# A two-layer decoder on one core: weight loads in slots, first keys in their own bank, VectorE's normalisation behind both maxima

## The reference

```python
# self-attention, per sequence (128 tokens), 16 heads of width 8
q, k, v = x @ Wq + bq, x @ Wk + bk, x @ Wv + bv
o   = softmax(q k^T / sqrt(8)) v @ Wo + bo
# attention over the past: queries from o, 2 x 256 past states, one softmax for each set
rq, rk, rv = o @ Wrq + brq, past @ Wrk + brk, past @ Wrv + brv
r   = mean over the two sets of softmax(rq rk^T / sqrt(8)) rv
g   = sigmoid([o, r] @ Wg + bg)
y   = layernorm(x + g * r + (1 - g) * o)
# then cross-attention, 16 experts of which the gates choose, gated attention unit,
# one-head attention, 8 experts of which one is chosen, each with a layer norm
```

## Time and profile before

| | us |
|---|---|
| median of 3 runs (875.06 to 891.75) | 875.5 |
| the profiled execution | 875.86 |
| its span | 874.1 |
| PE busy (71%) | 618.0 |
| DVE busy (60%) | 523.5 |
| ACT busy (40%) | 351.3 |
| POOL busy (14%) | 122.5 |

### The profile page before, as it was taken

One profiled execution on the slowest core, in us unless ns is written; L12 is line 12 of the kernel. 1 busy time (PEld: TensorE's weight loads), 2 busy tenths in 40 slices (PEclk: granted clock), 3 DMA queues, 4 the chain that ended last, 5 costly groups with the idle time before them and its releaser, 6 DMA issues.

```text
span 874.1 us, 16404 instructions
## 1 busy us (share of the span) xinstructions
PE 618.0 (71%) x5566; PEld 335.9 (38%) x5566; DVE 523.5 (60%) x1268; ACT 351.3 (40%) x642; POOL 122.5 (14%) x224
## 2 busy tenths in 40 slices
PE   1367887878677776777855777766999677686763
PEld 0144553223222222222322555543444366564552
DVE  2245664666656566565435576556656599667666
ACT  1035553465555465654743454540000223254221
POOL 4011210501010101101122120020000133110000
PEclk9999896699989899898976898956999899798796
DMA  4654220100010000000112222000000000010001
GB/s 128 196 140 106 54 59 1 38 2 1 1 38 2 1 20 18 3 1 1 38 37 67 56 74 76 8 0 1 0 0 0 1 0 1 0 32 12 1 0 48
DMA packets 35404, 27.63 MB, mean 32 GB/s; under 512 B 5894, under 2 KB 34310, under 8 KB 35206
## 3 DMA queue, kind: packets, MB, share of 16 engines
q1 hardware_dynamic: 35340, 26.77, 11.3%
HBM read 8.93 MB, written 1.05 MB: 11 GB/s over the span
## 4 chain that ended last, share of the span: by engine, by line
PE 54%; DVE 16%; issue 13%; ACT 10%; SPq 4%; DMA 1%; DVEq 1%; POOL 0%; ACTq 0%; POOLq 0%
PE banks L1008 8%; PE banks L1492 6%; PE banks L950 5%; PE banks L481 4%; PE banks L990 3%; PE banks L400 3%; ACT probs L617 3%; DVE rec_negmax L1167 3%; SPq L2086 2%; ACT o_T L1102 2%; PE banks L1019 2%; PE banks L1475 2%; PE banks L466 1%; PE banks L1554 1%; DVE o L1184 1%
## 5 line engine op out<-in xcount | busy, mean ns | idle before, releaser
L1167 DVE TENSOR_REDUCE rec_negmax<-banks 128x2 bf16<-128x512 f32 x256 | 167.4, 688 | 106.9 <-PE banks L950 106.4
L1095 ACT ACTIVATE probs<-banks 128x1024 f32<-128x1024 f32 x128 | 131.5, 1027 | 58.7 <-PE banks L990 58.6
L745 DVE TENSOR_REDUCE negmax<-banks 128x8 bf16<-128x1024 f32 x64 | 78.3, 1223 | 85.7 <-PE banks L443 85.5
L1008 PE MATMUL banks<-probs,rV 128*32 128x256 f32 x1024 | 88.7, 420 | 19.8 <-ACT o_T L1102 18.9
L617 ACT ACTIVATE probs<-banks 128x1024 f32<-128x1024 f32 x64 | 65.1, 1017 | 59.8 <-PE banks L466 59.8
L950 PE MATMUL banks<-shared 62*128 62x512 bf16 x256 | 63.5, 422 | 5.3 <-DVE rec_negmax L1167 5.3
L1492 PE MATMUL banks<-shared,w_r 128*128 128x512 f32 x128 | 64.5, 595 | 1.6 <-DVE shared L1525 1.5
L1525 DVE TENSOR_TENSOR shared<-banks,out_T 128x512 f32<-128x512 f32 x64 | 43.6, 690 | 23.4 <-PE banks L1475 23.4
L990 PE MATMUL banks<-shared 64*128 64x256 bf16 x512 | 52.2, 282 | 2.6 <-DMA shared<-rec_neg_T 2.6
L481 PE MATMUL banks<-probs,shared 128*32 128x128 f32 x1024 | 44.6, 296 | 12.0 <-ACT probs L617 11.9
L443 PE MATMUL banks<-shared 62*128 62x128 bf16 x512 | 28.8, 239 | 28.4 <-issue 11.8
(11 more groups left out here) (254 smaller groups left out, 1148.0 us busy)
## 6 DMA issues: line engine op xcount, KB each, us to landing
shared<-qk_parts SPq DMA_DIRECT2D x96, 128.0 KB, 2.4
shared<-rq_parts SPq DMA_DIRECT2D x30, 128.0 KB, 2.5
xk_T<-in_x_T SPq DMA_DIRECT2D x4, 256.0 KB, 3.3
w_r<-in_w_r SPq DMA_DIRECT2D x1, 1024.0 KB, 5.0
shared<-rec_neg_T SPq DMA_DIRECT2D x64, 2.0 KB
xk_T<-in_ctx_T SPq DMA_DIRECT2D x4, 256.0 KB, 3.1
kv_T<-in_ctx_T SPq DMA_DIRECT2D x16, 64.0 KB, 1.8
out<-Y SPq DMA_DIRECT2D x4, 256.0 KB, 2.4
```

Of the source, the lines that this page charges most:

```text
L745: nc.vector.tensor_reduce(c.negmax[:, i % 2, :].rearrange("p (r j) -> p r j", r=2)[:, :, 4 * half:4 * half + 4], c.max_pair.rearrange("p ( ...
L1008: last = self.nc.tensor.matmul(c.ctx_bank[HV * q:HV * (q + 1), past * PAIR:(past + 1) * PAIR], c.rV[:, t, 4 * g + q, :], c.probs[:, i % 4, ...
L1095: nc.scalar.activation(c.probs[:, i % 4, :], c.score_pairs[i % 2], ACT.Exp, scale=HEAD_SCALE)\
L1167: self.nc.vector.tensor_reduce(out, c.max_banks[r].rearrange("p (a t) -> p a t", a=NP_PAST), AX_X, ALU.max, negate=True).then_inc(s["rec_m ...
```

## The change

It does the following.

- **SyncE and ScalarE issue the loads.** load_first keeps two loads (w_qk, b_qk). Four (ident_b, w_v, b_v, ident_f) go to ScalarE's queue as load_turn; TensorE waits for them only ahead of its step loop. The rest is cut in slots of SyncE's step loop, behind rows, queries or keys of a step: load_past (6) in t = 0, load_out (4) in t = 1, three of load_rest's 33 in each of t = 2 to 12 (w_r, 1 MB, in t = 6; gate_rows, 512 KB, in t = 7), and Y (1 MB, still counted in load_rest) in t = 13. rows(0) comes behind load_past.
- **The first group.** The first keys are projected into score_banks[0], without a wait for the queries' bank. ScalarE and VectorE split all of the queries ahead of the keys, and ScalarE issues the six DMAs of the first keys itself. A small Exp on ScalarE and a memset on VectorE stand ahead of them.
- **Slots.** The past keys move from t = 2 to t = 6 (their spread on SyncE from t = 4 to t = 8), the past values from t = 3 to t = 12, the preparation from t = 12 to t = 13; waits are renamed to fit. The two small biases of halves() move to t = 5.
- **VectorE's order.** In the attention steps normalise(t-3) now stands ahead of window(t-1). In the loop over the past both maxima of a step come first, and normalise stands behind them at k = 2, 6, 10, 14 instead of between them at k = 3, 7, 11, 15; add_residual the same at k = 13 instead of 14.

```diff
+def split_bank(c, name, g):
+
+    return c.score_banks[0] if g == 0 and name in ("self_k_", "cross_k_") else c.proj_bank
...
     def project_out(g, *waits):
         pe.wait_ge(*s.after("self_ctx_t", 4 * g + 4))
+        if g == 0:
+            pe.wait_ge(*s.after("load_out", c.n_load_out * 16))
...
     def past_keys():
-        project("past_", 0, c.w_rk[:, :], c.past_T[:, :], ("load_rest", c.n_load_rest * 16), ("self_k_rest", 2))
+        project("past_", 0, c.w_rk[:, :], c.past_T[:, :], ("load_past", c.n_load_past * 16), ("self_k_rest", 3))
 
     def past_values():
-        pe.wait_ge(*s.after("past_rest", 1))
+        pe.wait_ge(*s.after("self_out", 2))
...
-            project_q(t // 4 + 1, *([("past_v", 1)] if t == 4 else [("self_out", t // 4 - 1)] if t > 4 else [("self_k_rest", 1)]))
+            project_q(t // 4 + 1, *([("self_k_rest", 2)] if t == 4 else [("self_out", t // 4 - 1)] if t > 4 else [("self_q_rest", 1)]))
         if t % 4 == 1 and t < 12:
             project_k(t // 4 + 1, ("self_q_rest", t // 4 + 2))
-        if t == 2:
+        if t == 6:
             past_keys()
-        if t == 3:
+        if t == 12:
             past_values()
         if t == 10:
             project_rq(0, ("self_k_rest", 4))
-        if t == 12:
+        if t == 13:
             prepare_pe(c, pe)
         if t == 14:
             project_rq(1, ("prep_d", 1))
         if t in (7, 11):
-            project_out(t // 4 - 1, ("rq_rest", 1) if t == 11 else ("self_k_rest", 3))
+            project_out(t // 4 - 1, ("rq_rest", 1) if t == 11 else ("past_rest", 1))
...
         project_k(0, ("rec_exp", 16 * NPAIR))
-        turn_x(0, ("cross_k_rest", 1))
+        turn_x(0)
         project_q(0)
         turn_x(1, ("cross_q_rest", 1))
     else:
         pe.wait_ge(*s.after("load_first", c.n_load_first * 16))
         project_q(0)
-        project_k(0, ("self_q_rest", 1))
+        project_k(0)
+        pe.wait_ge(*s.after("load_turn", c.n_load_turn * 16))
...
     else:
         act.wait_ge(*s.after("load_first", c.n_load_first * 16))
         high_of("q", 0, 0)
+        middle_act(c, act, "self_q_", 0, c.qk_parts[:, 0], c.left[:, 0, :])
         high_of("k", 1, 0)
-        middle_act(c, act, "self_q_", 0, c.qk_parts[:, 0], c.left[:, 0, :])
         middle_act(c, act, "self_k_", 0, c.qk_parts[:, 1], c.left[:, 1, :])
+        act.wait_ge(*s.after("set_zero", 2))
+        spread_rows(c, act, "self_k_", 0, c.KT[:, 0], c.qk_parts[:, 1], K_ORDER, "self_kt0")
...
+        if t == 5:
             halves()
+        if t == 6:
             rest(c, dve, "past_", 0, c.b_rk[:, 0:1], c.rq_parts[:, 3], c.left[:, 2, :])
-        if t == 3:
+        if t == 12:
             past_v()
-        if t == 12:
+        if t == 13:
             prepare_dve(c, dve)
...
         low_dve(c, dve, "cross_q_", 0, c.qk_parts[:, 0], c.left[:, 0, :])
     else:
         rest_of("q", 0, 0)
+        low_dve(c, dve, "self_q_", 0, c.qk_parts[:, 0], c.left[:, 0, :])
         rest_of("k", 1, 0)
-        low_dve(c, dve, "self_q_", 0, c.qk_parts[:, 0], c.left[:, 0, :])
         low_dve(c, dve, "self_k_", 0, c.qk_parts[:, 1], c.left[:, 1, :])
     for t in range(LAST + 1):
         if t < B:
             maximum(t, 0)
-        if t:
-            window(t - 1)
         if cross and 0 <= t - 4 < B:
             add_out(t - 4)
         if 0 <= t - 3 < B:
             normalise(t - 3)
+        if t:
+            window(t - 1)
         if t < B:
             maximum(t, 1)
             add_v_bias(t)
...
     load(0)
-    if not cross:
-        others(0)
-    load(1)
-    load(2)
     if cross:
+        load(1)
+        load(2)
         keys(0)
         queries(0)
     else:
+        others("first")
+        load(1)
         sp.wait_ge(*s.after("set_zero", 2))
         queries(0)
-        keys(0)
-        others(1)
+        others("rows")
     for t in range(B + 2):
         if 0 <= t - 1 < B:
             rows(t - 1)
@@ -907,11 +918,15 @@
             queries(t // 4 + 1)
         if t % 4 == 3 and t < 12:
             keys(t // 4 + 1)
+        if others:
+            others(t)
+        if t == 0 and not cross:
+            load(2)
         if t == 4:
             load(3)
         if t == 14 and not cross:
             past_queries_sp(c, sp, 0)
-        if not cross and t == 4:
+        if not cross and t == 8:
             spread_rows(c, sp, "past_", 0, c.rKT, c.rq_parts[:, 3], K_ORDER, "past_kt")
...
                 if more:
                     self.maximum(0)
-                if k == 3 and n:
-                    self.normalise(n - 1, 3)
-                if k in (7, 11, 15):
-                    self.normalise(n, k // 4 - 1)
-                if k == 14 and n:
-                    self.add_residual(n - 1)
                 if more:
                     self.maximum(1)
+                if k == 2 and n:
+                    self.normalise(n - 1, 3)
+                if k in (6, 10, 14):
+                    self.normalise(n, k // 4 - 1)
+                if k == 13 and n:
+                    self.add_residual(n - 1)
...
-    pe.wait_ge(*s.after("self_out", 2))
+    pe.wait_ge(*s.after("past_v", 1))
...
+        load_first = [(c.w_qk, "w_qk"), (c.b_qk, "b_qk")]
+        load_turn = [(c.ident_b, "ident_b"), (c.w_v, "w_v"), (c.b_v, "b_v"), (c.ident_f, "ident_f")]
+        load_past = [(c.past_T, "past_T"), (c.w_rk, "w_rk"), (c.b_rk, "b_rk"), (c.w_rv, "w_rv"), (c.b_rv, "b_rv"),
+                     (c.b_g, "b_g")]
+        load_out = [(c.w_o, "w_o"), (c.b_o, "b_o"), (c.w_rq, "w_rq"), (c.b_rq, "b_rq")]
+        load_rest = [(c.ln_w, "ln_w"), (c.w1_raw, "w1_raw"), (c.b1_raw, "b1_raw"), (c.w_g, "w_g"),
...
+                if step == "first":
+                    load_all(sp, load_first, "load_first")
+                elif step == "rows":
+                    sp.wait_ge(*s.after("set_zero_rest", 3))
+                    sp.dma_start(c.KT[63:P:64], a["key_rows"]).then_inc(s["load_rows"], 16)
+                    for past in range(NP_PAST):
+                        sp.dma_start(c.rKT[62 + past:P:64], a["past_rows"][past]).then_inc(s["load_rows"], 16)
+                elif step == 0:
+                    load_all(sp, load_past, "load_past")
+                elif step == 1:
+                    load_all(sp, load_out, "load_out")
+                elif step < 13:
+                    load_all(sp, load_rest[3 * (step - 2):3 * (step - 1)], "load_rest")
+                elif step == 13:
+                    sp.dma_start(c.Y[:, :, :], a["x"].rearrange("b t d -> t b d")).then_inc(s["load_rest"], 16)
...
+            load_all(act, load_turn, "load_turn")
+            act.wait_ge(*s.after("set_warm", 1))
+            nc.scalar.activation(c.warm[:, 1:2], c.warm[:, 0:1], ACT.Exp)
```

More of the change, by code:

```diff
@@ L290, in declare @@
     c.sem = s = Signals(lambda name: ctx.enter_context(nc.semaphore(name)))
-    s.own("load_", "first rest rows")
-    s.own("set_", "memset zero zero_rest bias")
+    s.own("load_", "first turn past out rest rows")
+    s.own("set_", "memset zero zero_rest bias warm")
     s.own("past_", "proj hi rest mid lo kt v_proj v")
@@ L349, in rest @@
         dve.wait_ge(*s.after(name + "lo", g))
[L350 removed]
+    nc.vector.scalar_tensor_tensor(left, split_bank(c, name, g), bias, parts[:, 0, :], ALU.add, ALU.subtract)\
         .then_inc(s[name + "rest"], 1)
@@ L399, in project @@
             pe.wait_ge(*s.after(name_, count))
-        nc.tensor.matmul(c.proj_bank, w, x, start=True, stop=True).then_inc(s[name + "proj"], 1)
+        nc.tensor.matmul(split_bank(c, name, g), w, x, start=True, stop=True).then_inc(s[name + "proj"], 1)
     def project_q(g, *waits):
@@ L727, in halves @@
     def halves():
-        dve.wait_ge(*s.after("load_rest", c.n_load_rest * 16))
+        dve.wait_ge(*s.after("load_past", c.n_load_past * 16))
         nc.vector.tensor_scalar(c.b_rv_half[:, :], c.b_rv[:, :], 0.5, None, ALU.mult).then_inc(s["set_bias"], 1)
@@ L852, in attention_pool @@
             residual(4 * g + 7)
-        if not cross and g == 1:
+        if not cross and g == 2:
             middle_low_pool(c, pool, "past_", 0, c.rq_parts[:, 3], c.left[:, 2, :])
```

32 lines of the change are left out of this document (9 added, 23 removed).

## The result

| | before | after |
|---|---|---|
| median of the runs, us | 875.28 | 808.76 (805.01 to 825.70, 4 runs) |
| ratio of the two, with its 95% interval | | 0.925 [0.917, 0.933] |
| profiled execution, us | 875.86 | 807.19 |
| its span, us | 874.1 | 805.4 |

The account below looks back on a forecast made before the run. No engine was full; TensorE's waits set the time. Savings of 16.3 us in self-attention, 38 of loop idle time, 4 of clock and 1.5 in cross-attention summed to 60, taking 875.86 to 816 us, range 802 to 838.

Parts of the forecast that it names:

- Idle time: Loop over the past: of 45.4 us TensorE idles waiting for normalise and add_residual, 38 go (bounds 19 and 45).
- The clock: Loop over the past: less time at TensorE's low clock, 4 us less (0 to 13).
- the clock recovers: Rival, 13%: all ten low-clock stretches in the loop go, 9 us more, and Y lands in 5.5 us: 805 us.
- First maxima: Start of self-attention: the first maxima come 4.7 us earlier (ends 1.5 and 6), at 17.0 us.
- the contention rival: Rival, 8%: spreads and loads share DMA engines; first keys land 3 us later, step 8's another 2: 821 us.
- The idle 16.92: Self-attention, before the first scores: TensorE's 16.92 us idle, with the first row issued behind loads, goes entirely.
- Past keys out of step 2: Self-attention: the past keys' 1.91 us of matmul leave the path in step 2, 1.2 us less.
- Steps 4 to 8: Self-attention: step 4 0.5 us less, normalise in step 5 0.6 less, the wait for spreads in step 8 2.0 more.
- SyncE's three issues fill its own slack: Self-attention, step 12: three load issues on SyncE use time it has spare, 0.3 us more.
- The wait for Y: Self-attention, step 13: the preparation waits for Y's load, about 4.2 us (3.5 to 5), then one low-clock step, 1.1.
- normalise ahead of rest: Self-attention, steps 5, 9 and 15: TensorE's idle time before the turned product goes, 0.6 us each.
- The slower rival: Rival, 3%: in the loop VectorE stands still in normalise for a late turned context, next maxima queued behind: 916 us.

Follow-up runs that it names:

- Experiment 2: Three variants of the changed kernel's loop: normalise in its old slot ahead of both maxima, 809.78 us; only add_residual moved, 852.41; one normalise of four put back, 828.98.
- experiment 1: Kernel before with only the loop's order changed, 828.34 us; with only attention's normalise moved, 872.25; changed kernel with both orders undone, 869.67.
- Experiment 4: Changed kernel with the first keys' spreads on SyncE's queue, 810.76 us; changed kernel with the past keys' six loads moved to step 1, 813.36.
- the last kernel of experiment 2: Changed kernel with one of four normalise per pair put back between the loop's maxima: 828.98 us in one execution.
- the third kernel of experiment 1: Changed kernel with both VectorE reorderings undone, leaving loads, slots and the first group: 869.67 us, ratio 0.993.
- experiment 3: Changed kernel with Y given its own semaphore, which VectorE waits for at the first add_residual: 808.60 us, ratio 0.922.

## Why the prediction held in sum and missed in its terms

**The loop: 58.7 against 42.** The mechanism was right: normalise and add_residual wait ready-made behind a maximum, and moving them frees the turn. Two terms were too small. *Idle time.* "Of 45.4 us idle in 34 places I leave ... 38 less" failed: 51.0 went. Of the 7 us left for gaps and late maxima only 1.1 is there. And 7.0 more came from a wait that the sum did not hold, the context's product waiting for ScalarE's copy (18.9 to 11.9): 37.9 + 7.5 - 1.1 + 7.0 = 51.3. Experiment 2 ties it to normalise: it stays at 18.9 where only add_residual is moved, is 12.8 with one turn of four late and 11.9 with none. ScalarE's waits before show a way that this can come about (before, then after):

```profile
ACT rec_neg_T L1108 <- PE banks L969: 41.5, 29, 1.5
```

```profile
ACT rec_neg_T L1123 <- PE banks L984: 2.3, 7, 0.4
```

ScalarE stood waiting 41.5 us for the turned maxima, and its exponentials and the copy of the context were queued behind that. That this queue is the way it goes is argued from the rows, not tried. *The clock.* 4 us was taken, with 13 as the end; 7.7 came. The line of the granted clock in 40 slices of the span, before and after, shows it:

```profile
PEclk9999896699989899898976898956999899798796
```

```profile
PEclk9988878599999999999569989569999999697896
```

The loop lies in slices 9 to 20 before, and four of these have an 8. After, slices 9 to 19 are nines throughout. The objection in the rival "the clock recovers", that the low stretches follow the gate product and not a wait, fell: in experiment 1 the low stretches inside the loop went with the waits alone, and in experiment 2 the busy time went up by 3.75 us with eight waits put back.

**Self-attention: 8.9 against 16.3**, by the steps of the prediction:

- *First maxima*, 4.7 less: 2.6 (21.70 to 19.13). ScalarE's queue was priced by its issues, 0.63 each, and these took 0.67. The first maxima were taken as 3.2 us behind the start of the last issue (2.6, and 0.6 for SyncE's loads), and it was 5.1 (14.03 to 19.13). The start at 19.13 is 2.1 later than the 17.0 forecast, where the contention rival had 3. Experiment 4 gives 1.5 for the order with everything on SyncE's queue; what part of it is the second queue is open.
- *The idle 16.92* went entirely, as forecast: 27.2 became 10.2 between first maxima and first scores.
- *Past keys out of step 2*, 1.2 less: by step 4 the gain was 62.96 - 43.07 = 19.9, which leaves 0.3 for it in this pair of profiles (2.0 with the last kernel of experiment 2, whose step 4 is at 41.40). TensorE comes earlier to step 4 and waits there, 4.18 us for 1.12. The prediction named this end for past values in step 3 and should have applied it to step 2 as well.
- *Steps 4 to 8*: 3.0 given back, where 0.9 was forecast (-0.5 - 0.6 + 2.0). TensorE waited 1.76 us at 65.63 for a row, which it did not before, and 4.01 for the spreads in step 8 against 3.36. The waits of 4 us are followed by a step at the low clock (eight products in 0.61 us, not 0.40), here in step 4 too, where the kernel before had 0.40.
- *Steps 8 to 12*: 1.0 given back against a gain of 0.3. The load of cos held SyncE for 2.23 us at 86.56, and the wait at step 12 is 4.19 us for 1.05. "SyncE's three issues fill its own slack" failed there. A load in that place took 1.4 to 1.9 us in the three kernels of experiment 2 too, with waits of 4.1 to 4.2 behind it; in the third kernel of experiment 1 none did, and the wait is 2.17.
- *Step 12 to the loop*: 6.9 given back against 5.9 (1.2 + 5.3 - 0.6).
- *The wait for Y*, 4.2 and 1.1 for the cold step (0.7 + 6.3 - 2.65 is 4.35, so the sum had slipped by 0.15): 5.09, and by experiment 3 it is worth 4.8 with all that follows. Y landed 6.6 us after its issue (6.3 taken).
- *normalise ahead of rest*, 1.8 less: 4 to 6 by itself. The prediction read one wait of 0.65 us and counted three steps; the row over all of self-attention has 6.4 us in 10 places, and 0.7 in one is left. With the loads moved the same waits go (6.0 in 10 places without the order, 0.7 in one with it), but the loop's beginning does not show it: 150.2 without the order lies among the 149.9 to 152.9 with it. So what this order is worth beside the loads is not settled.

**Cross-attention**, 1.5 less: 1.5. **The slower rival** did not come: VectorE waits in normalise for the turned context in 4 places, 9.9 us in total, as many and as long as before, and its wait for the maxima's matmuls fell from 97.4 us in 108 places to 36.5 in 73.

## What to carry to other kernels

An engine that works in order should take a short operation that others wait for ahead of the next long one, and the gain is read from the wait of the engine whose order sets the loop. Here it was more than that wait: 34 waits of 1.3 us were 45 us idle and gave 58.7, since another wait shrank with them and the clock rose. A load that gates anything should have a semaphore of its own, and a queue that carries rows on the critical path should have nothing put ahead of them that is not due: 9.6 to 12.7 us of the start hung on that, by the scatter of the mark. A single profile of each version does not measure a few microseconds: the same code moved its mark by 3.

## What the hardware showed that was not expected

- Short waits cost TensorE's clock: with 34 waits of up to 1.4 us in 288.6 us the granted clock was 0.93, with these gone 0.98. Put back in eight places they cost 1.6 us each for 1.2 us of idleness. Eight of them raised TensorE's busy time as much (3.75 us) as 28 did (3.4). The levels seen are 1.2 and 2.4 GHz (0.50 and 1.00).
- With the first keys on a second issuing queue, and SyncE's rows and loads beside them instead of behind, the first maxima came 1.5 us later (19.1 against 17.6), with the DMA engines at 1.00 instead of 0.74.
- A single DMA issue took 2.23 us on SyncE where its neighbours took 0.43, and six spreads 4.75 us (4.94 in the kernel before) where others took 3.8.
- The last 70 to 85 us of the program, the same matmuls, ran at a granted clock of 0.79 in one kernel's profile and 0.52 in another's, 14.5 us apart in TensorE's busy time.
- The same code of self-attention reached the loop at 149.9 to 152.9 us in four profiles.
